# Graph-attention first stage: the maximum over partitions goes through HBM, row statistics and transposes change their place

## The reference

```python
x = x + _L0_gnn_ref(_layernorm(x), adj, L0_gnn_W, L0_gnn_a)
x = x + _L0_ffn_ref(_layernorm(x), ...)
x = x + _L1_gnn_ref(_layernorm(x), adj, L1_gnn_W, L1_gnn_a)
x = x + _L1_ffn_ref(_layernorm(x), ...)

def _L0_gnn_ref(x, adj, W, a):
    h = jnp.einsum('bnf,fg->bng', x, W)
    f_src = h @ a[:F, 0]
    f_dst = h @ a[F:, 0]
    e = jax.nn.relu(f_src[:, :, None] + f_dst[:, None, :])
    att = jnp.where(adj > 0, e, NEG)
    att = jax.nn.softmax(att, axis=2)
    h_prime = jnp.einsum('bnm,bmf->bnf', att, h)
    return jax.nn.elu(h_prime)
```

## Time and profile before

| what | value |
|---|---|
| median of 3 runs | 2038.49 us (2036.75 to 2040.1) |
| the profiled execution | 2038.51 us, span from first to last instruction 2036.8 us |
| busy in the span | PE 1193.0, PEld 1024.5, DVE 1123.9, ACT 995.4, POOL 896.0 us |
| PE's granted clock, mean | 0.762 of full speed |
| first stage | to about 520 us of the span |

### The profile page before, as it was taken

One profiled execution on the slowest core, in us unless ns is written; L12 is line 12 of the kernel. 1 busy time (PEld: TensorE's weight loads), 2 busy tenths in 40 slices (PEclk: granted clock), 3 DMA queues, 4 the chain that ended last, 5 costly groups with the idle time before them and its releaser, 6 DMA issues. The chain is left out here.

```text
span 2036.8 us, 29795 instructions
## 1 busy us (share of the span) xinstructions
PE 1193.0 (59%) x10139; PEld 1024.5 (50%) x10139; DVE 1123.9 (55%) x2503; ACT 995.4 (49%) x1416; POOL 896.0 (44%) x725
## 2 busy tenths in 40 slices
PE   2767676641667762267675666777312206999970
PEld 2656666631556651155554555566212205999860
DVE  2765666552333333579898898999531222343323
ACT  3555555421444431188766866976312204666640
POOL 1011545476355564125325325432467662656550
PEclk8787877765777786578887887888555557999995
DMA  7532332112444443321212111210111125555518
GB/s 240 195 126 84 127 126 86 45 44 94 138 129 128 132 122 104 133 84 73 84 64 74 73 70 68 94 64 32 34 36 46 37 91 155 163 169 163 164 56 247
DMA packets 166117, 213.61 MB, mean 105 GB/s; under 512 B 29812, under 2 KB 121102, under 8 KB 164944
## 3 DMA queue, kind: packets, MB, share of 16 engines
q1 hardware_dynamic: 147792, 175.99, 27.7%
q0 software_dynamic: 18176, 35.72, 5.1%
HBM read 156.71 MB, written 58.56 MB: 106 GB/s over the span
## 5 line engine op out<-in xcount | busy, mean ns | idle before, releaser
L555 POOL DMA_INDIRECT y_dram<-f_ys,f_Xb x312 | 318.0, 1019 | 262.7 <-DVE f_ys L576 180.5
L1469 ACT ACTIVATE g_near<-g_s_row,g_steep 128x1024 fp8e4<-128x1024 f32 x352 | 369.3, 1134 | 2.3 <-issue 2.3
L1444 PE MATMUL g_bp<-g_G,g_near 128*128 128x102 bf16 x4096 | 247.6, 233 | 175.1 <-DVE g_near L1361 175.0
L1444 PEld LDWEIGHTS g_bp<-g_G,g_near 128*128 128x128 fp8e4 x4096 | 239.8, 113 | 203.3 <-issue 201.8
L204 POOL DMA_INDIRECT xs_dram<-r_row,r_pos x256 | 268.4, 1048 | 120.4 <-issue 80.2
L622 PE MATMUL f_ops<-f_w,f_g 128*128 128x128 f32 x1872 | 272.3, 290 | 42.1 <-ACT f_g L658 28.9
L622 PEld LDWEIGHTS f_ops<-f_w,f_g 128*128 128x128 f32 x1872 | 259.0, 204 | 68.8 <-ACT f_g L658 38.4
L658 ACT ACTIVATE f_g<-f_hps,f_ex 128x512 f32<-128x512 f32 x234 | 159.2, 689 | 199.4 <-PE f_hps L614 103.7
L1361 DVE TENSOR_TENSOR g_near<-g_near,g_mask 128x2048 uint32<-128x2048 uint32 x64 | 163.5, 2555 | 50.1 <-ACT g_near L1469 27.5
L1350 DVE TENSOR_SCALAR g_near<-g_s_row,g_nd 128x1024 fp8e4<-128x1024 f32 x160 | 158.3, 1038 | 0.0
L945 PE MATMUL attout<-V,Pt 128*128 128x129 f32 x1024 | 146.9, 304 | 9.5 <-DVE Pt L814 8.5
(11 more groups left out here) (223 smaller groups left out, 2164.1 us busy)
## 6 DMA issues: line engine op xcount, KB each, us to landing
raw<-in_adj SPq DMA_DIRECT2D x64, 512.0 KB, 6.5
g_s_row<-rows_dram SPq DMA_DIRECT2D x64, 512.0 KB, 3.6
f_Xb<-xs_dram SPq DMA_DIRECT2D x78, 288.0 KB
f_w<-in_L_ffn_W SPq DMA_DIRECT2D x78, 256.0 KB
f_yb<-y_dram SPq DMA_DIRECT2D x16, 1024.0 KB, 6.1
f_w<-in_L_ffn_W SPq DMA_DIRECT2D x78, 128.0 KB
mask_dram<-mask SPq DMA_DIRECT2D x16, 512.0 KB, 3.5
g_mask<-mask_dram SPq DMA_DIRECT2D x8, 1024.0 KB
```

Of the source, the lines that this page charges most:

```text
L555: pool.indirect_dma_start(y_d.rearrange("n k d -> (n k) d"), bass.IndirectOffsetOnAxis(ap=Xb[:, i % XB, r, D:D + 1].bitcast(U32), axis=0), ...
L1444: ins = pe.matmul(bp[h % 2][:, t // 4, (t % 4) * 6 * C:(t % 4 + 1) * 6 * C], near[:, h % 4, j, t * P:(t + 1) * P], G[:, s, j, h, :, :], st ...
L1469: ins = act.activation(near[:, h % 4, j, :], s_row[:, h % 4, :], ACT.Relu, scale=STEEP, bias=steep[:, s, j, h:h + 1], saturate=False)
```

## The change

Three things in `phase_gat0`, with the line numbers of the changed kernel 1 to 7 higher than before.

1. The maximum over partitions: SP stores `dmax[:, 0:1]` (128 values) to a tensor in HBM, waits for it, and loads it back so that every partition holds all 128 values (`dall`, 128x128). DVE reduces that (L850). GpSimd's operation goes.
2. `dve_statistics` moves from the start of a step (after the first weights) to the end of the step before, after `update_negative`; `dve_shift` moves ahead of the clips; on GpSimd `pool_roots` moves from the start of a step to between the two groups of indirect stores.
3. `act_normalise` moves from slot 2 to slot 0 of the eight slots of a step, `pe_transpose` from 3 to 2, `pe_logits` from 5 to 4, `act_evacuate` from 4 to the head of 3, `act_logits` to the head of 5.

```diff
@@ sync
+                sp.wait_ge(s_dm, b + 2)
+                sp.dma_start(dmax_dram[b + 1].rearrange("(p o) -> p o", o=1), dmax[:, 0:1]).then_inc(s_dst, 16)
+                sp.wait_ge(s_dst, 16 * (b + 2))
+                sp.dma_start(dall[:, :], dmax_dram[b + 1:b + 2, :].to_broadcast([P, P])).then_inc(s_dld, 16)
                 for hf in range(2):
                     sp.wait_ge(s_mask, (b + 1) * NT + 4 * (hf + 1))
@@ gpsimd
-            def largest(c):
-                hold(pool, (s_dm, c + 1))
-                pool.partition_all_reduce(dmax[:, 1:2], dmax[:, 0:1], P, K["rmax"]).then_inc(s_dM, 1)
...
-                if 0 <= r < B:
-                    R.pool_roots(pool, r)
                 if q >= 0:
                     R.pool_scatter(pool, q, 0)
-                if prepare:
-                    if b < B - 2:
-                        deviation(b + 2)
-                    largest(b + 1)
+                if b < B - 2:
+                    deviation(b + 2)
+                if done:
+                    R.pool_roots(pool, b - 1)
@@ vector
             def negate_largest(c):
+                dve.wait_ge(s_dld, 16 * (c + 1))
+                dve.reduce_max(dmax[:, 1:2], dall[:, :], AX.X).then_inc(s_dM, 1)
                 dve.wait_ge(s_dM, c + 1)
...
-                if 0 <= r < B:
-                    dve.wait_ge(s_up, 2 * r + 2)
-                    R.dve_statistics(dve, r)
                 if done:
                     finish(b - 1, 1 - s, 2)
+                if 0 <= r < B:
+                    R.dve_shift(dve, r)
                 if prepare:
                     clip_adj(b + 1, 0)
-                if 0 <= r < B:
-                    R.dve_shift(dve, r)
...
                 if done:
                     update_negative(b - 1)
+                    dve.wait_ge(s_up, 2 * b)
+                    R.dve_statistics(dve, b - 1)
@@ tensor
-                    if t == 3 and 0 <= r < B:
+                    if t == 2 and 0 <= r < B:
...
-                    if t == 5 and 0 <= r < B:
+                    if t == 4 and 0 <= r < B:
                         R.pe_logits(pe, r)
@@ scalar
+                    if t == 3 and 0 <= r < B:
+                        R.act_evacuate(act, r, 0)
+                        R.act_evacuate(act, r, 1)
+                    if t == 5 and 0 <= r < B:
+                        R.act_logits(act, r)
...
-                    if t == 2 and 0 <= r < B:
+                    if t == 0 and 0 <= r < B:
                         act.wait_ge(R.s_k, 2)
                         R.act_normalise(act, r)
                     if t == 4 and 0 <= r < B:
-                        R.act_evacuate(act, r, 0)
-                        R.act_evacuate(act, r, 1)
                         R.act_copy(act, r)
-                    if t == 5 and 0 <= r < B:
-                        R.act_logits(act, r)
```

More of the change, by code:

```diff
@@ L686, in phase_gat0 @@
     dmax = sb("dmax", [P, 2], FP32)
+    dall = sb("dall", [P, P], FP32)
+    dmax_dram = K["dmax_dram"]
     ndmax = sb("ndmax", [P, 1], FP32)
@@ L725, in phase_gat0 @@
     s_dm, s_dM, s_nd = sem("g0_dm"), sem("g0_dM"), sem("g0_nd")
+    s_dst, s_dld = sem("g0_dst"), sem("g0_dld")
     s_hs, s_hsum = sem("g0_hs"), sem("g0_hsum")
@@ L1526, in build @@
         K["rows_dram"] = nc.dram_tensor("rows_dram", (B, 8, N), FP32, kind="Internal").ap()
+        K["dmax_dram"] = nc.dram_tensor("dmax_dram", (B, P), FP32, kind="Internal").ap()
         K["xs_dram"] = nc.dram_tensor("xs_dram", (ROWS, RW), FP32, kind="Internal").ap()
```

## The result

The changed kernel takes 2074.11 us in the median of 4 runs (2069.80 to 2074.71), the kernel before 2037.62 us beside it (4 runs, 2033.33 to 2040.10): a ratio of 1.018, 95% interval 1.016 to 1.021. The forecast was 2036.5 within 2023 to 2049. It was wrong: the kernel is 36 us slower. The profiled execution spans 2072.9 us. Its last indirect store of the first stage ends at 548.2 us, against 513.9 before: 34.3 of the 36 us lie in the stage that was edited.

A forecast was written before the change was run, and what follows sets the result against it. In the edited first stage, DVE's work and its waits for the maximum, factors F and prefix copy bound the kernel, GpSimd the tail. Prologue +13, step gains and tail growth summed to -2.0 from 2038.51: 2036.5 us, range 2023 to 2049.

The forecast's parts named there:

- W0(0): Prologue's end, where batch 0's first-half weights start on DVE: at 65 instead of 52.03 us, +13 (bounds 10 to 15).
- steps 0 and 1: First two steps of the first stage: round trip about 3 us shorter than GpSimd's reduction, PE chain shorter, -1.3 us.
- W0 to W1: From a batch's first-half weights to its second-half weights on DVE: 19 us, nothing gained; 21.2 in steps 4 to 7.
- W1 to W0: From a batch's second-half weights to the next batch's first-half weights: 29.0 us instead of 32.6, bounds 28.4 and 33.
- step 3: From batch 3's first weights to batch 4's: 19.2 + 32.6 us becomes 18.9 + 29.0, -3.9.
- 284.1 to 356.2: From batch 5's first-half weights to batch 6's second-half weights: 72.1 us becomes 21.2 + 29.0 + 21.2, -0.7.
- 356.2 to 392.7: From batch 6's second-half weights to batch 7's first-half weights: 36.5 us becomes 28.3, no batch left to normalise, -8.2.
- tail: After batch 7's second-half weights, GpSimd alone decides: two roots between store groups +5.8, way between batches' stores +0.4, together +6.2.
- W1+19.9: Round-trip load's landing, counted from a batch's second-half weights; DVE asks at 19.1, leaving 0.6 us of waiting per step.
- Rival B: Steps 2 to 6: round trip takes 10 us instead of 7, sharing queue and DMA engines, +14; 2050 us, chance 0.25.
- A: Steps and prologue: PE's signals not late, round trip covered, prologue at its low bound; 2025 us, chance 0.20.
- C: Prologue: its store isn't held up, first weights stay near 55 us, -10; 2027 us, chance 0.08.

The follow-up runs named there:

- the trip alone: The kernel before with the round trip through HBM in place of GpSimd's reduction, nothing moved: 1984.0 us, ratio 1.011.
- the moves alone: The changed kernel with the maximum over partitions back on GpSimd, the moves kept: 1983.5 against 1961.3 us, ratio 1.012.
- an early maximum: The changed kernel with the maximum over partitions on PE instead of the round trip, all three moves kept: 1944.8 us, ratio 0.992.
- the second profile: The changed kernel unedited, run again on another chip: 2069.3 against 2026.4 us, ratio 1.020.

## Why the prediction was wrong

The forecast by its own terms, against the two profiled executions (the marks of the earlier trace rows and those above):

| term | forecast | measured | off by |
|---|---|---|---|
| prologue, W0(0) | +13 | +16.3 (52.03 to 68.3) | +3.3 |
| steps 0 and 1 | -1.3 | +6.1 | +7.4 |
| step 2, W0 to W1 | -3.0 | -3.2 | -0.2 |
| step 2, W1 to W0 | -5.6 | -0.4 | +5.2 |
| step 3 | -3.9 | +0.2 | +4.1 |
| step 4 | -2.1 | +5.3 | +7.4 |
| 284.1 to 356.2 | -0.7 | +4.7 | +5.4 |
| 356.2 to 392.7 | -8.2 | -1.6 | +6.6 |
| step 7, W0 to W1 | +3.6 | +2.0 | -1.6 |
| tail | +6.2 | +4.9 | -1.3 |
| sum | -2.0 | +34.3 | +36.3 |

**The step that failed** is the pricing of the round trip: "About 1 us for the store behind them, 0.4 to issue and 3.5 for the load give W1+19.9, and 0.6 us is left". The store cost 7.3 to 9.8 us until its load was issued, the load 4.2, and 5.9 us were left. (By the prediction's own marks, W1+19.9 against W1+19.1, 0.8 was left, not 0.6; this changes nothing.) I took the price from the earlier trace rows, a store of 32 KB in rows of 512 bytes; this one has 128 elements of 4 bytes. The runs with 64 and 512 bytes a partition bring the store to 1.4 to 3.6 us and W1 to W0 to 28.0 to 28.3, so the rest of that sum held: the waits that go, the statistics that come in (3.0) and the reduction of `dall` (0.3 taken, 0.28 measured) were right. With the store at that price the kernel was 2 to 8 us slower than before (one run each), where the forecast was 2 faster: some 30 of the 36 us are this one price, the rest is in the terms below. The bound of 33 for W1 to W0 was too low as well (34.0 to 34.9). It lacked that what stands behind a late trip runs one after the other.

**Rival B** (2050) had the place right, and neither the size nor the reason: it allowed 10 us for the trip where 12 came, and put it down to shared queue and engines. Taking half of the loads out of its way changed nothing. The slow landing is there in steps 0 and 1 (7.3 and 7.8 us), before the first indirect store, and at 397.75 (8.0), after the last adjacency load. The rival that was missing is the size of the elements. The Trainium skill (DMA: Bandwidth & Descriptors, Specifications) warns of small transfers, though with a bound that these runs don't show. I weighed only its fixed 2.0 us per transfer (Anatomy of one DMA), which it gives for transfers issued from GpSimd while these are SP's; the 64-byte store comes near it and the 4-byte one does not. Rivals A and C, both faster, did not come: W0(0) was at 68.3, and the trip was covered in no step.

**The prologue** was 3.3 us under-sized for the same reason: issuing took 5.62 us, as the 6.3 of the earlier trace rows had said, but the landing came at 62.24 instead of 57 to 59; with 64 bytes it came at 56.5.

**Steps 0 and 1** were to gain from a trip 3 us shorter than the reduction. It was not shorter, and `dve_biases`, on which PE waits in step 1, now stands behind trip and statistics: W0(2) came 48.3 us after W0(1) instead of 42.8. PE waited 11.4 us for the biases where it had waited 6.4, 8.3 with the trip alone and 9.8 with the moves alone, and so these cost 2 and 3 us there.

**W0 to W1**: the mechanism was right (the wait for the prefix copy takes the statistics' place; the second group waits for the roots), its size short. The forecast was 21.2 in steps 4 to 6, measured 23.2, 23.5 and 19.2. Part of it comes from the late trip: the group started at W1+33.0 instead of W1+27.3. With an early maximum it started at W1+27.4 and W0 to W1 was 22.2, so this part is 1 us. The other part is the landing, reckoned as 1.5 to 2 us after the last store. In step 4 the group ends at 260.43 and the rows start at 266.48, 6.05 us later:

```profile
258.88 1.02 ACT L1027 ACTIVATE mask<-adjT 128x1024 fp8e4<-128x1024 bf16 x1 [6.52 <-PE adjT L955]
266.48 1.66 ACT L387 ACTIVATE r_row<-x_sb,r_nb,r_pwo 128x128 f32<-128x128 f32 x4 [4.88 <-DMA xs_dram<-r_row,r_pos]
```

ACT waits 4.88 us for it, where I had put +1. The other thing that I had put into this term, a first mask late by 3.3 us, did not come: the mask starts at 258.88, W0+8.0, as it would without it. That 21.2 came near 23.2 is partly luck.

**Right** were step 2's first half, the growth of the tail from two roots between the store groups (4.9 for 6.2; 4.27 and 3.15 us lie between the groups where 0.3 did), and that GpSimd's 6 to 7 us of preparation vanish: the gate at 260.43 follows the last store of its group without idle time, where the earlier trace rows show 7.49.

That the moves lose by themselves while the maximum is late I had not seen at all. In the forecast they stood beside an early maximum. Even there steps 4 and 5 are 2.4 to 3.2 us longer with them than without, and their gain of about 10 us comes from steps in which they let PE reach the maximum sooner. Behind a late maximum they lengthen the chain maximum, statistics, roots, stores, landing, rows, prefix copy, in which each link waits for the one before.

## What to carry to other kernels

Price a transfer by a row with the same bytes per element, not only with the same total: in the steps a store of one float a partition took 7.3 to 9.8 us to land, one of 16 floats 1.4 to 3.3. Before a round trip or any long wait is put into a strictly ordered engine, look at what stands behind the wait and doesn't need its result: moving 4.2 us of such work ahead of it gave back three quarters of the loss at no cost. And judge a set of moves with the bound that it will run under, step by step: the same moves cost 22 us with the maximum on GpSimd and gained about 10 with it on PE, where they shortened steps 2, 3 and 6 and lengthened most others.

## What the runs showed of the hardware

- A store of 128 x 4 bytes to HBM lands after 7.3 to 9.8 us in the steps (7.0 to 10.1 over all runs), also at 397.75 us, when no adjacency load is under way (8.0); 128 x 64 bytes after 1.4 to 3.3. The store's packets are through after 1.1 us, its sixteen semaphore increments come from 2.1 to 8.0 us. Why is not settled: it vanishes somewhere between 4 and 64 bytes, or with the words' distance in HBM.
- One row of 512 bytes spread to 128 partitions lands after 2.8 us, own rows after 1.8.
- Indirect stores land up to 6.5 us after the last instruction of a group in the steps (7.2 in the second profile), but 1.4 in the tail (the group's end at 494.6, rows from 496.07), where no adjacency is loaded.
- In step 3 of the run with the moves alone GpSimd was idle for 6.03 us before its reduction and 6.68 before the power operation behind it (the roots), with nothing in the profile to wait for. Both vanish when the reduction leaves GpSimd.
